# The last of sixteen batches in two more PSUM banks, its attention gathered by matrix products, its end on VectorE

## The reference, cut to what matters

```python
x = x + L0_xattn(ctx, ctx, layernorm(x), ssm_kernel, D, 8)   # long convolution, 16 heads of 8
x = x + L0_ffn(layernorm(x), ...)                            # 8-bit activations, ternary weights
x = x + L1_xattn(layernorm(x), ctx, mask, mask, ...)
x = x + L1_ffn(layernorm(x), ...)

# L1_xattn: 16 heads of 8 channels, softmax over the 256 positions of ctx
dot  = einsum('bhdt,bhds->bhts', q, k) / sqrt(8)             # then masked
amap = softmax(dot, axis=-1) * mask
out  = einsum('bhts,bhds->bhdt', amap, v)

# L1_ffn: per channel row, the 32 largest of 512 logits
logits = xn @ Wc.T / temperature
top_vals, top_idx = top_k(logits, 32)
expressed = softmax(top_vals) @ genes[top_idx]               # 32 numbers
out = tanh(expressed @ Wd.T) * xn * (expressed @ Wu.T) * scale
```

## Time and profile before

| | us |
|---|---|
| median of 3 runs | 581.97 |
| lowest and highest of them | 581.94, 582.58 |
| the profiled execution, its own time | 580.47 |
| its span in the trace | 578.7 |
| TensorE, VectorE busy in the span | 463.3, 453.2 |
| GpSimd, ScalarE busy in the span | 377.2, 350.3 |

### The profile page before, as it was taken

One profiled execution on the slowest core, in us unless ns is written; L12 is line 12 of the kernel. 1 busy time (PEld: TensorE's weight loads), 2 busy tenths in 40 slices (PEclk: granted clock), 3 DMA queues, 4 the chain that ended last, 5 costly groups with the idle time before them and its releaser, 6 DMA issues.

```text
span 578.7 us, 11242 instructions
## 1 busy us (share of the span) xinstructions
PE 463.3 (80%) x3587; PEld 258.3 (45%) x3587; DVE 453.2 (78%) x885; ACT 350.3 (61%) x607; POOL 377.2 (65%) x692
## 2 busy tenths in 40 slices
PE   1686699997987988888989889898887888777452
PEld 1575477765754544444544344443443333322110
DVE  4586479998669979799899899798988997874341
ACT  1469524333121677788788788788876786776231
POOL 6467389998977757777778778776664762343222
PEclk9888889999879999999899999899999998996755
DMA  6970110101551257357354573546745765210100
GB/s 197 372 174 19 48 28 29 22 7 56 89 120 24 80 79 163 94 99 150 91 102 124 100 144 100 90 120 127 157 103 111 137 143 96 50 24 19 50 9 19
DMA packets 93935, 54.49 MB, mean 94 GB/s; under 512 B 16611, under 2 KB 93603, under 8 KB 93877
## 3 DMA queue, kind: packets, MB, share of 16 engines
q1 hardware_dynamic: 93876, 53.78, 41.0%
HBM read 35.84 MB, written 17.42 MB: 92 GB/s over the span
## 4 chain that ended last, share of the span: by engine, by line
PE 24%; issue 21%; POOL 20%; POOLq 14%; DVE 7%; ACT 6%; DMA 4%; SPq 3%; DVEq 0%; ACTq 0%
PE pair L280 7%; POOL kv L949 5%; PE bank L501 4%; POOL w_raw L1026 4%; ACT cT L1310 3%; POOLq L977 3%; POOLq L42 3%; DVE w_int L1656 2%; POOL w_int L45 2%; POOLq L975 2%; PE pair L488 2%; PE bank L393 2%; PE pair L472 2%; DMA yT<-in_x 2%; POOLq L40 2%
## 5 line engine op out<-in xcount | busy, mean ns | idle before, releaser
L1656 DVE TENSOR_REDUCE w_int<-pair 128x4 f32<-128x1024 f32 x128 | 155.2, 1213 | 28.9 <-PE pair L472 28.3
L1310 ACT ACTIVATE cT<-pair 128x1024 f32<-128x1024 f32 x128 | 131.0, 1023 | 38.2 <-PE pair L488 35.8
L280 PE MATMUL pair<-kv,toep 128*128 128x256 f32 x384 | 102.8, 413 | 11.7 <-POOL kv L949 8.0
L280 PEld LDWEIGHTS pair<-kv,toep 128*128 128x128 f32 x384 | 76.0, 207 | 28.2 <-issue 8.4
L488 PE MATMUL pair<-w_raw,KS 57*128 57x256 bf16 x512 | 51.2, 279 | 33.7 <-ACT cT L1310 23.7
L949 POOL TENSOR_TENSOR kv<-cT 128x512 f32<-128x512 f32 x64 | 66.2, 1041 | 17.9 <-PE pair L280 12.4
L501 PE MATMUL bank<-cT,v_aug 128*32 128x256 f32 x1024 | 73.4, 406 | 0.2 <-ACT qT L1318 0.2
L1481 DVE TENSOR_TENSOR prod<-pair,qT 128x512 f32<-128x512 f32 x64 | 43.8, 685 | 23.5 <-PE pair L280 22.7
L472 PE MATMUL pair<-KS,w_raw 54*128 54x256 bf16 x512 | 50.3, 275 | 11.2 <-DVE w_int L1656 10.8
L488 PEld LDWEIGHTS pair<-w_raw,KS 57*128 57x128 bf16 x512 | 16.9, 95 | 72.9 <-ACT cT L1310 54.1
L1257 ACT ACTIVATE w_raw<-bank,st 128x512 f32<-128x512 f32 x32 | 22.0, 688 | 39.0 <-PE bank L394 39.0
(11 more groups left out here) (174 smaller groups left out, 941.9 us busy)
## 6 DMA issues: line engine op xcount, KB each, us to landing
w_raw<-scr_q SPq DMA_DIRECT2D x32, 192.0 KB
KS<-scr_k SPq DMA_DIRECT2D x32, 192.0 KB
scr_q<-w_int SPq DMA_DIRECT2D x16, 192.0 KB, 2.5
scr_k<-w_int SPq DMA_DIRECT2D x16, 192.0 KB, 2.6
scr_o<-qT SPq DMA_DIRECT2D x64, 36.0 KB
yT<-in_x SPq DMA_DIRECT2D x4, 512.0 KB, 7.6
ctx_all<-in_ctx SPq DMA_DIRECT2D x4, 512.0 KB, 8.1
x_b<-in_x SPq DMA_DIRECT2D x16, 128.0 KB, 4.9
```

Of the source, the lines that this page charges most:

```text
L280: mm = pe.matmul(bank[:, lh * n:(lh + 1) * n], toep[:, h, (lh - sh) * P:(lh - sh + 1) * P], rhs[:, sh, :], start=(sh == 0), stop=(sh == lh))
L1310: act.activation(probs[g % 4].rearrange("p j l -> p (j l)"), SC[:], ACT.Exp).then_inc(s("scores_free"), 1)
L1656: dve.tensor_reduce(neg_max[:, :, 2 * g:2 * g + 2].rearrange("p t j -> p j t"), M[:].rearrange("p (j t s) -> p j t s", t=KL, s=L), AX.X, A ...
```

## The change

For batch 15 alone (`LAST`):

- `scores` alternates between the pairs `SC` and `M`, and waits for the exponential of two groups back instead of the last one.
- TensorE gathers the heads. `gather_attention` multiplies each quarter of `o_quad` with two selecting matrices of 128x32 (made from the identity by GpSimd, `make_selectors`), one that picks the 8 rows of sums, one that picks the denominator row eight times; both results go to bank `X6`. VectorE masks the sums, inverts the denominators (256 per row), multiplies and adds. None of the DRAM steps is done for this batch, nor are GpSimd's `add_attention` and the two steps on `den32`.
- The weights are one VectorE product: (struck-out logits are at most GONE) times the exponentials. ScalarE's exponential of the leftovers and GpSimd's difference are left out.
- `down_up` is two products of 256 columns, the down half in `X7` first, then the up half in `X5`. VectorE does the last three steps: up times `xr`, times the tanh, plus `x3`.

```diff
+        selectors = inside("ctx_all", [P, 2, 4 * HD])
...
+        LAST = B - 1
+        sc_banks = (SC, M)
...
+        def score_bank(b, g):
+            return sc_banks[g % 2] if b == LAST else SC
...
+                if b == LAST:
+                    pe.wait_ge(s("max_free"), GRP * B)
                 if b or g:
-                    pe.wait_ge(s("scores_free"), GRP * b + g)
+                    pe.wait_ge(s("scores_free"), GRP * b + (max(g - 1, 0) if b == LAST else g))
...
-                        mm = pe.matmul(SC[:, at:at + L], KS[b % 3][rows, g, sh * P:(sh + 1) * P], QS[b % 3][rows, g, :],
+                        mm = pe.matmul(score_bank(b, g)[:, at:at + L], KS[b % 3][rows, g, sh * P:(sh + 1) * P], QS[b % 3][rows, g, :],
...
+            def gather_attention(b, q):
+                if b != LAST:
+                    return
+                if q == 0:
+                    take6("attention", b)
+                    pe.wait_ge(s("selectors_ready"), 2)
+                pe.wait_ge(s("o_free"), turn_o["values", b, q])
+                to = slice(32 * q, 32 * q + 32)
+                pe.matmul(X6[to, L:2 * L], selectors[:, 1], o_quad[:, q, :],
+                          start=True, stop=True)
+                pe.matmul(X6[to, 0:L], selectors[:, 0], o_quad[:, q, :], start=True, stop=True
+                          ).then_inc(s("attention_gathered"), 1)
...
-                pe.matmul(X7[:], exprT, wduT[:], start=True, stop=True).then_inc(s("down_up_filled"), 1)
+                if b != LAST:
+                    pe.matmul(X7[:], exprT, wduT[:], start=True, stop=True).then_inc(s("down_up_filled"), 1)
+                    return
+                pe.matmul(X7[:, 0:L], exprT, wduT[:, 0:L], start=True, stop=True).then_inc(s("down_up_filled"), 1)
+                take5("up", b)
+                pe.matmul(X5[:, 0:L], exprT, wduT[:, L:2 * L], start=True, stop=True).then_inc(s("down_up_filled"), 1)
...
                 expressed(m - 11)
                 scores(m - 8, 4)
                 values(m - 8, 1)
+                gather_attention(m - 8, 0)
...
                 scores(m - 8, 6)
                 maxima(m - 7, 6)
                 values(m - 8, 2)
+                gather_attention(m - 8, 1)
                 scores(m - 8, 7)
                 maxima(m - 7, 7)
                 transpose_xr(m - 9)
                 values(m - 8, 3)
+                gather_attention(m - 8, 2)
+                gather_attention(m - 8, 3)
                 transpose_hidden(m - 2)
                 project_v(m - 6)
 
...
             def write_attention(b):
-                if not live(b):
+                if not live(b) or b == LAST:
...
+            def make_selectors(b):
+                if b != LAST:
+                    return
+                by_head = ident[:].rearrange("p (j e) -> p j e", e=32)
+                for n, rows in enumerate((by_head[:, :, 0:HD], by_head[:, :, HD:HD + 1].broadcast_to([P, 4, HD]))):
+                    pool.tensor_copy(selectors[:, n].rearrange("p (j d) -> p j d", d=HD), rows).then_inc(
+                        s("selectors_ready"), 1)
+
...
             def exp_left(b):
-                act.wait_ge(s("best_struck"), 4 * (b + 1))
-                act.activation(e_left, left, ACT.Exp, bias=col(b, NB), scale=temp_scale[:, 0:1])
+                if b == LAST:
+                    act.wait_ge(s("best_found"), 4 * (b + 1))
+                else:
+                    act.wait_ge(s("best_struck"), 4 * (b + 1))
+                    act.activation(e_left, left, ACT.Exp, bias=col(b, NB), scale=temp_scale[:, 0:1])
                 act.activation(best_e[:], best[:], ACT.Exp, bias=col(b, NB), scale=temp_scale[:, 0:1],
...
+            def attention_masked(b):
+                if b != LAST:
+                    return
+                k = b % 2
+                dve.wait_ge(s("attention_gathered"), 4)
+                dve.wait_ge(s("x3_ready"), b - 1)
+                dve.tensor_tensor(o_nat[k], X6[:, 0:L], mask_b[b % NC][:], ALU.mult).then_inc(s("attention_scaled"), 1)
+
+            def attention_inverses(b):
+                if b != LAST:
+                    return
+                dve.wait_ge(s("attention_gathered"), 4)
+                dve.wait_ge(s("x3_ready"), b - 1)
+                dve.reciprocal(o_den[b % 2], X6[:, L:2 * L]).then_inc(s("attention_scaled"), 1)
+
+            def attention_scaled(b):
+                if b != LAST:
+                    return
+                k = b % 2
+                dve.wait_ge(s("attention_scaled"), 2)
+                dve.tensor_tensor(o_nat[k], o_nat[k], o_den[k], ALU.mult).then_inc(s("attention_scaled"), 1)
+
+            def attention_added(b):
+                if b != LAST:
+                    return
+                dve.wait_ge(s("attention_scaled"), 3)
+                dve.wait_ge(s("res_ready"), b - 2)
+                dve.tensor_tensor(x3[b % 3], x2[:, b % 6, :], o_nat[b % 2], ALU.add).then_inc(s("x3_ready"), 1)
...
+            def choose_last(b):
+                if b != LAST:
+                    return
+                dve.wait_ge(s("exs_ready"), b + 1)
+                dve.wait_ge(s("best_struck"), 4 * (b + 1))
+                dve.wait_ge(s("wT_filled"), b)
+                dve.scalar_tensor_tensor(w_top, left, GONE, e_all, ALU.is_le, ALU.mult).then_inc(s("w_ready"), 1)
+
+            def up_times_xr(b):
+                if b != LAST:
+                    return
+                dve.wait_ge(s("rs_ready"), b + 1)
+                dve.wait_ge(s("down_up_filled"), b + 2)
+                dve.wait_ge(s("res_ready"), b)
+                dve.scalar_tensor_tensor(dxu, X5[:, 0:L], col(b, RS), xr[b % 3], ALU.mult, ALU.mult).then_inc(
+                    s("x5_free"), 1)
+
+            def times_down(b):
+                if b != LAST:
+                    return
+                dve.wait_ge(s("down_ready"), b + 1)
+                dve.wait_ge(s("x5_free"), turn5["up", b])
+                dve.tensor_tensor(dxu, dxu, down, ALU.mult).then_inc(s("dx_ready"), 1)
+
+            def last_sum(b):
+                if b != LAST:
+                    return
+                dve.wait_ge(s("dx_ready"), b + 1)
+                dve.wait_ge(s(f"res{b % 2}_out"), 16 * (b // 2))
+                dve.tensor_tensor(res[b % 2][:], dxu, x3[b % 3], ALU.add).then_inc(s("res_ready"), 1)
...
                 top_next(m - 11, 2)
+                attention_masked(m - 10)
+                attention_inverses(m - 10)
+                attention_scaled(m - 10)
+                attention_added(m - 10)
                 gather_x3(m - 10)
...
                 down_times_up(m - 12)
+                up_times_xr(m - 12)
+                times_down(m - 12)
+                last_sum(m - 12)
                 maxima(m - 8, 7)
...
                 top_strike(m - 11, 3)
+                choose_last(m - 11)
                 scale_x(m - 1)
```

23 lines of the change are left out of this document (12 added, 11 removed).

## The result

The changed kernel takes **576.77 us** (median of five runs, 575.80 to 579.03) against 581.97 for the kernel before (five runs, 580.42 to 582.66). The ratio is 0.9919, with a 95% interval of 0.9890 to 0.9948: 5.2 us less. The forecast was 577.0, in a range from 574.0 to 579.8.

The account below looks back on a forecast made before the run. No engine is full; the serial last 60 us bound the kernel. Gains of 2.65 + 1.86 + 1.22 = 5.7 us, or 4.1 with the late clock, were taken as 5.0, giving 577.0 us, range 574.0 to 579.8.

Parts of the forecast that it names:

- leg 1: 519.06 to 537.07, batch 15's scores and values up to batch 14's logits; claimed those logits at 536.5, 0.6 us earlier.
- late clock: TensorE back at 2.4 GHz only at 531.2, not 527.8; batch 14's logits then near 538.1, 1.0 us late.
- Leg 2: 537.07 to 549.62, batch 15's attention to the end of its moments; claimed their end at 546.97, 2.65 us earlier.
- Leg 3: 549.62 to 566.29, to the end of batch 15's last strike, with VectorE's wait of 2.52 us; claimed no gain.
- Leg 4: 566.29 to 568.92, exponentials, difference and transpose of batch 15; one VectorE product instead was to gain 1.86 us.
- Leg 5: 568.92 to 576.48, through the last sum; split down_up and VectorE's last three steps were to gain 1.22 us.
- two clocks: TensorE at 2.4 GHz again from 527.8, gain 5.7 us, or only from 531.2, gain 4.1 us.
- VectorE eats the attention: Rival: a reciprocal of 2.4 us and late gathers leave leg 2 no gain; 579 us, chance 0.14.
- The clock gives more: Rival: TensorE's clock rises during batch 15's logits, gain 7 to 8.5 us in all; 574 us, chance 0.16.
- The slower case: Rival: TensorE stays at 1.2 GHz, batch 14's logits come 5.9 us late; 584.5 us, chance 0.05.

## Why the prediction was right, point by point

The time was right, 577.0 for 576.77, and so was the side. The steps fared differently, and the closeness of the sum is in part luck.

- **The base.** The prediction counted on one trace of the kernel before. It holds 4.3 us that the second trace of the same kernel doesn't, 3.0 of them in leg 1, with TensorE at 1.2 GHz. The earlier trace rows leave out the second of that leg's two low stretches (1.94 us of values for 1.07), and the prediction sets its own values at the full clock without counting that. Each leg below is therefore set against both.
- **Leg 1** was to put the logits of batch 14 17.4 us after the first scores (536.5), or 19.0 with a late clock. They came after 16.23, since this trace's dip was shorter. With the clock back after 8.6 us (8.7 had been assumed) the leg took 17.34 in a later trace, so the list was added up well. The sentence that "the second pair buys more than 2 us and the gathers spend most of it" was nearly right in kind: 1.8 bought (some 1.4 at the same clock), 2.6 spent. What the text didn't see is how much the clock alone does: without pair and gathers the same leg takes 15.04 or 18.01 us, and with both 15.15 to 18.58.
- **Leg 2** was to end 28 us after the first scores, 2.65 sooner. It ended after 26.27, which is 4.3 sooner than in the first trace and 1.2 sooner than in the second. Its length from the logits was worked out well: 10.5 us forecast, 10.04 measured, 12.45 or 12.55 before. But the step that credited a gain of 2.65 to legs 1 and 2, for taking DRAM's two stops out of the path, named the wrong earner. At the same clock the gathers and VectorE's attention are worth nothing (41.85 and 41.82 us to the last strike), and without the second pair they cost 0.77. What is gained up to the moments is the pair's, and against the second trace of the kernel before it is 1.2 us, not 2.65.
- **The rows that were priced from neighbours** held. The reciprocal of 256 numbers a row took 1.75 us (1.74 forecast); the Trainium skill's repeat count of 8 ("VectorE: DVE Perf Modes", "First, the fixed hardware budget") had led to an estimated 2.1, and the measurement decides. A gather's two products start 0.43 us apart and the next work 0.53 behind, 0.96 in all (0.86 forecast); the last two gathers together took 1.64 (1.72 forecast). GpSimd's copies for the selectors took 0.35 us, in a pause of which 1.45 us were left.
- **Leg 3** was to gain nothing, with the wait of 2.52 us. The wait was 1.71, since the clock rose at the end of the logits of batch 15 (3.58 us for 3.78) and stayed up for the transposes of batch 14's weights behind them (0.63 for 1.09). The second trace of the kernel before has 1.30, so this isn't the change's work either. The leg takes 15.64 us, beside 16.67 and 15.44 before.
- **Leg 4** was to save 1.86: 1.79 in the traces and 1.80 in the run without it. ScalarE's exponential lies beside the strike, as said.
- **Leg 5** was to save 1.22: it saved 1.06. My gaps between the three VectorE steps were too small; the leg is 3.69 us and not 3.53.
- **The sum** of 5.0 stood between two clocks. The whole traces, second of the kernel before and change, give 3.9. That the sum fits the medians (5.2) better than its terms deserve is in part luck: legs 1 and 2 brought 1.2 us minus the 0.2 of leg 3, for 2.65 or 1.06 forecast, and some 1.3 of the 5.2 stands in no trace.
- **The rivals.** "VectorE eats the attention" named a real thing, a list in which the new steps wait behind batch 14, but with the wrong price: the reciprocal isn't 2.4, and legs 4 and 5 stand. "The clock gives more" was shown to be there for the taking, but the change doesn't take it: behind the 6 us pause the logits of batch 15 still need 3.58 us. The slower case would have needed 1.2 GHz throughout leg 1, and no trace has that; three have it for 10 us, and leg 1 then took 18.6.

Still open is how much of the 5.2 us between the medians each part brings. Executions of one kernel lie 10 us apart or more (576.71 to 590.21 in 35 runs), the ratios of the kernels with one part undone don't show even the parts of 1.8 us, and so the parts above are read from one trace each, counted from the same event. Why the stretch ahead of the first scores differs from one execution to the next (519.06 and 524.17 for the same kernel) wasn't looked into.

## What to carry to other kernels

Undo each part of a change alone, and compare traces in which the clock was alike: the part that removed the most visible waits was worth nothing here, because its new work stood in front of the very operation on which the next leg depends. Parts undone one at a time need not add up. When a part brings an input forward, move its users forward too, on every engine's list, and look for the next wait each time (VectorE's list, then GpSimd's, then a bank). In a serial tail, TensorE's clock can be worth as much as the steps: with idle products it brought 2.3 us behind the logits of batch 14 (28.17 to 25.84). Those that ended 0.4 us ahead of the transpose of batch 15 held it in two traces, those that ended 1.7 us ahead did not in one.

## What the runs showed of the hardware

- TensorE's clock isn't the same in two executions of one kernel. In the kernel before it fell after the first scores of batch 15 in both traces, but was back some 7 us after them in one and 12 in the other; the tail took 53.13 and 57.42 us. The kernels with the change reached the logits of batch 14 between 15.15 us (no dip) and 18.58 (a dip of 10 us) after those scores.
- Idle bf16 products of 512 columns run at 0.22 us each (20 in 4.48). Eight, then 20 of them, ended up to 0.55 us ahead of the work, kept the clock at 1.00 to the last product, in two traces; 20 that ended 1.72 us ahead, in one trace, didn't keep it for the logits behind.
- The reciprocal on VectorE grows by 6.2 ns for each number in a row, from 1 (0.15 us) over 32 (0.35) to 256 (1.75). It is four times an ordinary operation of that size (0.42).
- Two fp32 products of 256 columns into the same 32 columns of the array start 0.43 us apart, as long as one takes by itself. When the next goes to other columns it starts 0.23 us behind (540.59 and 540.82 in the change), and the eight products of the values, spread over all columns, take 1.07 us together.
